# First attention: scores of the first tiles ahead of the value products, and batch two's six products in one round

## The reference

```python
mod = (_silu(L0_c) @ L0_wmod).reshape(2, 6, 1, -1)       # sa, ca, ga, sb, cb, gb
ga = (2 * (ga >= 0) - 1) * jnp.maximum(jnp.abs(ga), 0.25)
h = _layernorm(x) * (1 + ca) + sa
Q = h @ Wq.T + bq;  K = h @ Wk.T + bk;  V = h @ Wv.T + bv # 128 wide, one head
attn = softmax(where(causal, Q @ K.T / sqrt(128), -inf))
x = x + ga * (attn @ V)
```

## Time and profile before

| what | value |
|---|---|
| profiled execution, device time | 973.75 us |
| its span | 972.0 us |
| median of three runs | 973.2 us (969.73 to 974.66) |
| TensorE busy | 909.9 us, 94% |
| ScalarE, VectorE, GpSimd busy | 642.2, 593.1, 292.5 us |
| first attention, from the first q product to the last tile | 16.7 to about 82.5 us |

### The profile page before, as it was taken

The page is one execution under the profiler, slowest core; times in us unless marked ns, Lnnn a source line. Parts: engine busy times, 40 slices in busy tenths (PEclk is TensorE's granted clock), DMA queues, the critical chain, the costliest instruction groups (busy, mean ns, idle before and its releaser), DMA issues. The chain is left out here.

```text
span 972.0 us, 25390 instructions
## 1 busy us (share of the span) xinstructions
PE 909.9 (94%) x10211; PEld 668.2 (69%) x10211; DVE 593.1 (61%) x1355; ACT 642.2 (66%) x1094; POOL 292.5 (30%) x367
## 2 busy tenths in 40 slices
PE   7998897369999999999999999999999999998987
PEld 6676576146777767777776777777677777776776
DVE  5556111566666666666666666666666666677975
ACT  2552143158787878778787878778787877884442
POOL 5124800503224242422324142232414223215110
PEclk9998799569999999999999999999999999999999
DMA  8300701100020002002000200100020010000000
GB/s 251 137 2 22 254 26 52 40 1 2 2 90 3 2 2 92 2 2 84 9 3 1 91 2 2 76 17 2 2 91 1 3 31 10 3 1 2 1 23 22
DMA packets 27128, 35.48 MB, mean 37 GB/s; under 512 B 6042, under 2 KB 21716, under 8 KB 26836
## 3 DMA queue, kind: packets, MB, share of 16 engines
q1 hardware_dynamic: 25988, 31.76, 10.0%
q0 software_dynamic: 1024, 2.10, 0.7%
HBM read 28.48 MB, written 5.37 MB: 35 GB/s over the span
## 5 line engine op out<-in xcount | busy, mean ns | idle before, releaser
L552 DVE CUSTOM_DVE_ANT_0 soft<-SC,strips 128x1024 f32<-128x1024 f32 x256 | 303.3, 1223 | 79.7 <-PE SC L394 79.6
L513 ACT ACTIVATE soft<-soft,nmax 128x1024 f32<-128x1024 f32 x256 | 294.1, 1150 | 3.5 <-DVE nmax L552 3.4
L430 PE MATMUL CX<-PTs,V 128*64 128x256 f32 x2048 | 244.7, 381 | 0.0
L498 ACT COPY PTs<-PT 128x1024 f32<-128x1024 f32 x128 | 129.6, 1013 | 139.2 <-PE PT L413 139.2
L394 PE MATMUL SC<-qk 64*128 64x512 f32 x1536 | 212.5, 409 | 7.0 <-DVE nmax L552 6.9
L413 PEld LDWEIGHTS PT<-ident,soft 64*128 64x128 f32 x4096 | 159.0, 139 | 70.2 <-issue 28.9
L430 PEld LDWEIGHTS CX<-PTs,V 128*64 128x64 f32 x2048 | 142.6, 137 | 92.8 <-issue 35.0
L560 DVE COPY PTs<-PT 128x512 f32<-128x512 f32 x128 | 88.5, 692 | 161.0 <-PE PT L413 161.0
L413 PE MATMUL PT<-ident,soft 64*128 64x64 f32 x4096 | 176.4, 226 | 3.9 <-ACT PTs L505 2.4
L394 PEld LDWEIGHTS SC<-qk 64*128 64x128 f32 x1536 | 137.8, 188 | 32.9 <-issue 5.2
L341 POOL CAST qk<-raw_qk 128x512 fp32r<-128x512 f32 x60 | 36.8, 614 | 262.3 <-ACT raw_qk L317 262.3
(11 more groups left out here) (268 smaller groups left out, 998.2 us busy)
## 6 DMA issues: line engine op xcount, KB each, us to landing
strips<-bias_vec SPq DMA_DIRECT2D x8, 1920.0 KB, 7.0
arena<-in_L_ffn_w SPq DMA_DIRECT2D x1, 2048.0 KB, 11.3
slots_in<-arena SPq DMA_DIRECT2D x1, 1536.0 KB, 9.3
arena<-slots_in SPq DMA_DIRECT2D x8, 192.0 KB, 4.5
slots_out<-arena SPq DMA_DIRECT2D x8, 192.0 KB, 2.0
x<-in_L_attn_x SPq DMA_DIRECT2D x2, 512.0 KB, 4.4
out<-x SPq DMA_DIRECT2D x4, 256.0 KB, 2.3
arena<-in_L_wmod SPq DMA_DIRECT2D x2, 384.0 KB, 4.8
```

The lines of the kernel that those rows point to most:

```text
L430: ins = pe.matmul(CX[hd * DK:(hd + 1) * DK, 0:2 * P], V1[:, vb, t, hd * DK:(hd + 1) * DK], PTs[:, g % 2, hd, t, :], start=(t == 0), stop=( ...
L498: act.copy(turned_out(n, 0), turned_in(0)).then_inc(ev("ptA_out"), 1)
L513: act.activation(soft[:, n % RING, hd, :], soft[:, n % RING, hd, :], ACT.Exp, bias=nmax[:, j:j + 1], scale=-1.0, accum_out=rsum[:, hd, n % ...
L552: dve.tensor_tensor_reduce(soft[:, n % RING, hd, :], SC[hd][:, :], strips[:, u // B % 2, hd, i * P:i * P + S], 1.0, 3.4e38, ALU.add, ALU.m ...
```

## The change

- TensorE: scores 0, 1, 2, the transposes of tile 0, scores 3 and the transposes of tile 1 stand ahead of products 2 and 5 (both values of batch one). Products go in the order 0, 1, 3, 4, 2, 5, 6, ..., 11, and the waits of the other engines follow this order through `issued0`. Then come context 0, the transposes of tile 2, the row transposes of batch two, context 1, and products 6 to 11 in one go; from i = 5 on the loop is as before.
- Banks: product 2 goes to the fourth half bank instead of the first, product 9 to the third, 10 to PT[1], 11 to the second. Product 9 waits for the maximum of the third tile, 10 and 11 for the copies of q and k that were in their banks.
- The modulation helper is split in two. The vectors are made behind the first row transposes, not in front of them. ScalarE's row copy of the first half comes ahead of its copies of the vectors.
- Warm-up products: 3 instead of 6 behind the small rows' transpose, none instead of 4 behind the weights' transposes, none instead of 2 between the first two row transposes.
- VectorE: the modulation columns are copied ahead of the first normalised rows. Maxima 0 to 2, quarter three of the rows, maximum 3, quarter four, values 2 and 5, the additions of tiles 0 and 1, values 8 and 11, then the loop from i = 4.
- ScalarE: exponentials 0, 1, 2, copy of transposes 0, exponential 3, copies 1 and 2, then batch two's row copies and its q and k copies.

```diff
--- before.py
+++ after.py
@@ -230,9 +230,11 @@
 
 
         fills0 = [(kind, b, half) for b in range(B) for half in range(2) for kind in "qkv"]
-        fill_banks = [PT[0], PT[1], four_sc[0], CX[:, :], MI[:, :], four_sc[1],
-                      PT[1], four_sc[1], four_sc[3], PT[1], four_sc[1], four_sc[3]]
+        fill_banks = [PT[0], PT[1], four_sc[3], CX[:, :], MI[:, :], four_sc[1],
+                      PT[1], four_sc[1], four_sc[3], four_sc[2], PT[1], four_sc[1]]
         order0 = list(range(TB)) + list(range(NT - 1, TB - 1, -1))
+
+        issued0 = (0, 1, 3, 4, 2, 5, 6, 7, 8, 9, 10, 11)
 
         def width0(i):
 
@@ -840,7 +842,7 @@
                 for f, (kind, fb, half) in enumerate(fills0):
                     if kind == "v" or fb != b:
                         continue
-                    act.wait_ge(ev("proj0_full"), f + 1)
+                    act.wait_ge(ev("proj0_full"), issued0.index(f) + 1)
                     dst = (q0T if kind == "q" else k0T)[:, b * S + half * 512:b * S + half * 512 + 512]
                     if kind == "q":
                         ins = act.activation(dst, fill_banks[f], ACT.Identity, scale=-QK_SCALE, bias=cols[:, C_BQS:C_BQS + 1])
@@ -864,19 +866,25 @@
                 act.copy(tmp[:, at:at + width0(j) // P, :].rearrange("p k q -> p (k q)"),
                          PTW[:, 0:width0(j)]).then_inc(ev("pt0_out"), 1)
 
+            norm_out(0, (0,), (0,))
             mod_out(0)
-            norm_out(0, (0,))
+            norm_out(0, (0,), (1,))
             act.wait_ge(ev("bq_scaled"), 1)
             fills_out(0)
-            for i in range(NT + 2):
+            exp0(0)
+            exp0(1)
+            exp0(2)
+            turned0(0)
+            exp0(3)
+            turned0(1)
+            turned0(2)
+            norm_out(0, (1,))
+            fills_out(1)
+            for i in range(4, NT + 2):
                 if i < NT:
                     exp0(i)
-                if i >= 2:
+                if i >= 5:
                     turned0(i - 2)
-                if i == 2:
-                    norm_out(0, (1,))
-                if i == 3:
-                    fills_out(1)
                 if i == 14:
                     norm_out(1, (0,))
             norm_out(1, (1,))
@@ -1032,7 +1040,7 @@
                 kind, b, half = fills0[f]
                 t0 = b * TB + 4 * half
                 dve.wait_ge(ev("gate0_folded"), 1)
-                dve.wait_ge(ev("proj0_full"), f + 1)
+                dve.wait_ge(ev("proj0_full"), issued0.index(f) + 1)
                 tt(v0[:, t0:t0 + 4, :], fill_banks[f].rearrange("p (t d) -> p t d", d=D), bc_tiles(bvg[:, b, :], 4),
                    ALU.add).then_inc(ev("v0_out"), 1)
 
@@ -1066,14 +1074,12 @@
             silu()
             dve.wait_ge(ev("var_ready"), 1)
             inverse_roots(tiles(0))
+            mod_columns(0)
             rows_out(quarter(0), rows0)
-            mod_columns(0)
             rows_out(quarter(1), rows0)
             norm_stats(0, (1,))
             dve.wait_ge(ev("var_ready"), 2)
             inverse_roots(tiles(1))
-            values0(2)
-            rows_out(tiles(1), rows0)
             dve.wait_ge(ev("consts"), 8)
             ts(base_b, iota_c, 1.0 / P, None, ALU.mult).then_inc(ev("base_ready"), 1)
 
@@ -1119,16 +1125,23 @@
 
                 return bank[:, 0:n * E].rearrange("p (t e) -> p t e", e=E)
 
-            for i in range(NT):
+            biased0(0)
+            biased0(1)
+            biased0(2)
+            rows_out(quarter(2), rows0)
+            biased0(3)
+            rows_out(quarter(3), rows0)
+            values0(2)
+            values0(5)
+            added0(0)
+            added0(1)
+            values0(8)
+            values0(11)
+            for i in range(4, NT):
                 biased0(i)
-                if i == 1:
-                    values0(5)
-                if i >= 3:
+                if i >= 5:
                     added0(i - 3)
-                if i == 3:
-                    values0(8)
-                    values0(11)
-                if 4 <= i != 11:
+                if i != 11:
                     stats0(i - 4)
                 if i == 10:
                     stats0(7)
@@ -1367,27 +1380,28 @@
             keep_clock(PT[0], 6)
             pe.wait_ge(ev("ld_rows"), 16 * 8)
             pe.transpose(MI[:, 0:NROWS], rows[0:NROWS, :], ident[0:NROWS, 0:NROWS]).then_inc(ev("rows_turned"), 1)
-            keep_clock(PT[0], 6)
+            keep_clock(PT[0], 3)
             pe.wait_ge(ev("ld_w0"), 48)
             for n in range(3):
                 ins = pe.transpose(SC[0][:, n * P:(n + 1) * P], w0raw[:, n, :], ident[:, :])
             ins.then_inc(ev("w0_turned"), 1)
-            keep_clock(PT[0], 4)
-
-            def mod_rows(layer):
+
+            def mod_columns(layer):
 
                 for n, m in enumerate((0, 1, 3, 4)):
                     ins = mm(MI[:, 64 + 2 * n:66 + 2 * n], wmod[layer][:, m * D:(m + 1) * D], siluT[:, 2 * layer:2 * layer + 2],
                              start=True, stop=True)
                 ins.then_inc(ev("modc_full"), 1)
+
+            def mod_vectors(layer):
+
                 for b in range(B):
                     mm(four_sc[(2, 3, 1, 3)[2 * layer + b]], siluT[:, 2 * layer + b:2 * layer + b + 1].to_broadcast([P, P]),
                        wmod[layer][:, 2 * D:6 * D], start=True, stop=True).then_inc(ev("mod_full"), 1)
 
             pe.wait_ge(ev("silu_ready"), 1)
             pe.wait_ge(ev("ld_wmod"), 16)
-            mod_rows(0)
-            keep_clock(PT[0], 4)
+            mod_columns(0)
 
             def turn_rows(n, k):
 
@@ -1397,9 +1411,10 @@
                     ins = pe.transpose(rows_bank(n, k)[:, t * P:(t + 1) * P], rows_in[:, 4 * k + t, :], ident[:, :])
                 ins.then_inc(ev("h_turned"), 1)
 
+            keep_clock(PT[0], 4)
             pe.wait_ge(ev("w0T_ready"), 1)
             turn_rows(0, 0)
-            keep_clock(PT[0], 2)
+            mod_vectors(0)
             turn_rows(0, 1)
 
             def fill(f):
@@ -1407,12 +1422,16 @@
                 kind, b, half = fills0[f]
                 at = b * S + half * 512
                 pe.wait_ge(ev("hT_ready"), 2 * b + half + 1)
+                if f == 2:
+                    pe.wait_ge(ev("mod_copied"), 2)
                 if f == 8:
                     pe.wait_ge(ev("hT_ready"), 4)
                 if f == 6:
                     pe.wait_ge(ev("qk0_out"), 2)
-                if f >= 9:
-                    pe.wait_ge(ev("v0_out"), 3) if kind == "v" else pe.wait_ge(ev("qk0_out"), 5 if kind == "q" else 6)
+                if f == 9:
+                    pe.wait_ge(ev("nmax0"), 3)
+                if f >= 10:
+                    pe.wait_ge(ev("qk0_out"), f - 5)
                 if kind == "v":
                     pe.wait_ge(ev("gate0_folded"), 1)
                     for t in range(4):
@@ -1429,15 +1448,14 @@
                 if i == 0:
                     pe.wait_ge(ev("mod_copied"), 2)
                     pe.wait_ge(ev("qk0_out"), 2)
-                if i == 1:
-                    pe.wait_ge(ev("v0_out"), 1)
                 if i >= 2:
                     pe.wait_ge(ev("nmax0"), i - 1)
                 if i == 4:
-                    pe.wait_ge(ev("qk0_out"), 4)
-                    pe.wait_ge(ev("v0_out"), 4)
+                    pe.wait_ge(ev("qk0_out"), 7)
+                    pe.wait_ge(ev("v0_out"), 3)
                 if i == 5:
                     pe.wait_ge(ev("qk0_out"), 8)
+                    pe.wait_ge(ev("v0_out"), 4)
                 for k in range(0, w, 512):
                     m = min(512, w - k)
                     ins = mm(scores_bank0(i)[:, k:k + m], q0T[:, t * P:(t + 1) * P], k0T[:, b * S + k:b * S + k + m],
@@ -1458,6 +1476,7 @@
                 pe.wait_ge(ev("pt0_out"), j + 1)
                 if j < 2:
                     pe.wait_ge(ev("qk0_out"), j + 3)
+                    pe.wait_ge(ev("v0_out"), 1)
                 else:
                     pe.wait_ge(ev("att0_out"), j - 1)
                 n = width0(j) // P
@@ -1497,24 +1516,30 @@
                          skip_group_check=True)
                 ins.then_inc(ev("ranks_full"), 1)
 
-            for f in range(5):
+            for f in (0, 1, 3, 4):
                 fill(f)
-            for i in range(NT + 3):
+            for i in range(3):
+                scores0(i)
+            turn0(0)
+            scores0(3)
+            turn0(1)
+            fill(2)
+            fill(5)
+            context0(0)
+            turn0(2)
+            pe.wait_ge(ev("v0_out"), 2)
+            turn_rows(0, 2)
+            turn_rows(0, 3)
+            context0(1)
+            for f in range(6, 12):
+                fill(f)
+            for i in range(4, NT + 3):
                 if i < NT:
                     scores0(i)
-                if i == 1:
-                    fill(5)
-                if 2 <= i < NT + 2:
+                if 5 <= i < NT + 2:
                     turn0(i - 2)
```

(12 more changed lines are left out.)

## The result

The changed kernel takes 966.69 us in the median of six runs (965.64 to 968.43), the kernel before 972.46 (969.73 to 974.66, six runs). The ratio is 0.9942, with a 95% interval of 0.9925 to 0.996: 0.6% faster, 5.8 us. The profiled execution has 968.43 us in all and a span of 966.7, against 973.75 and 972.0.

What follows compares the result with a forecast made beforehand. TensorE's waits before the sixth tile's scores (the mark) were taken as the bound; moving the mark 4.9 us plus 0.25 later gave 5.15 off 973.75, 968.6, stated as 968.3 against the median. Likeliest range 966.5 to 970, wider 965.5 to 972.3.

Steps and rivals of the forecast that it cites:

- The bound: First attention: TensorE sets the pace from the sixth tile's scores (the mark, 39.76 us) to 80.60; before that it waits.
- The start: Opening: column products from 9.1 us, clock rising at about 15.5, vectors copied by 16.95, GpSimd's chain ending at 23.5.
- Scores ahead: First attention: scores 0 at 20.1 us, value products from 23.7, GpSimd wait hidden behind scores 0 to 3.
- VectorE as the new cover: Before batch two: VectorE is late next; quarter three 1.5 us, quarter four 1.06, values 2 and 5 done at 27.2.
- Banks: Products 9 to 11 do not wait; fifth tile's scores come at 33.9 us instead of behind VectorE's last copy, done at 34.8.
- The last term of the sum: Behind the mark: the fourth tile's transposes no longer wait 0.27 us for ScalarE, gaining 0.25 more.
- The shift one for one: A shift of the mark reaches the program's end in full; phases behind 80 us count nothing, 1.5 us allowed each side.
- The clock never rose as early as before: Opening, rival: the clock rises as before, the start is 1.3 us earlier, 967.0 us; chance 0.13.
- The fall in a new hole: TensorE between 22 and 27 us, rival: the clock falls in new holes, costing 1.7 us, 970.0; chance 0.11.
- Rows held by every GpSimd operation: VectorE's quarters three and four, rival: every GpSimd operation holds rows, 3.2 us more, 971.5; chance 0.10.
- Gain given back: Router and scatter, rival: the gain is lost as clock and queues shift, 973 us; chance 0.07.
- Slower: Opening, rival: without warm-ups TensorE stays at 1.2 GHz, 14 us lost less 5.15, 982 us; chance 0.07.

Runs made afterwards that it cites:

- the quiet kernel: Changed kernel with GpSimd's feed-forward gate made only after the sixth tile's maximum: 962.95 us, ratio 0.9952 to the kernel before.
- order only: Changed kernel with the old start and its warm-ups, keeping the new order of scores, products and banks: 965.63 us, ratio 0.9965 to the kernel before.
- the start alone: Kernel before with split modulation, fewer warm-ups, row copy and columns first, but old order and banks: 969.37 us, ratio 1.0009 to the kernel before.
- the slower comparisons: Groups of runs in which the kernel before takes 972 or 974 us; in the faster ones it takes 968 and 967.

## Why the prediction was right, point by point

**The number.** The forecast was 968.3, with 966.5 to 970 as the likeliest's own range; 966.69 was measured. Of the 1.6 us between them 0.7 is the kernel before, whose median is 972.46 over six runs and was 973.2 over three. The rest is the shift: 4.9 forecast, 5.8 measured, of which, as below, about 4.7 is the change's own.

**The bound.** Right: TensorE's pace from the mark on (38.95 of 40.71 us), waits before it. A shift of the mark did carry through; with its size see below.

**The start.** Right in kind, short in size. I had the rise of the clock at 15.5; it came at 16.9, the vectors ran slow to their end (3.58 instead of 2.7) and were copied at 17.58 instead of 16.95. That is the clock alone: the column products (8.98, forecast 9.1) and the vectors (13.38, forecast 13.5) began on time, although TensorE could turn the first small rows only at 6.50, against 5.95 before. GpSimd's chain took 6.5 as expected. Other executions were kinder: the five profiles of kernels with this start and these banks have the mark at 35.79, 35.42, 34.72, 34.12 and 35.00, mean 35.0 (the quiet kernel, which differs in GpSimd alone, has 34.92). The predicted 34.9 was right for the kernel, and 0.9 early for the execution that was shown.

**Scores ahead.** Right: scores 0 at 20.67 (20.1), value product at 24.25 (23.7), no wait on GpSimd. I had no wait for ScalarE's first copy as such; it is 0.67.

**VectorE as the new cover.** Right, and shown by the largest hole, 0.99, which VectorE releases. Quarter three took 1.83 (1.5), quarter four 1.10 (1.06), the two values end at 27.6 (27.2). That products of GpSimd hold the rows and tensor-scalar operations don't is shown by the quiet kernel (quarter three 1.71, four 1.03) and by order only (2.76 beside three products).

The Trainium skill, "SBUF — State Buffer", section "Who interferes with whom", counts a `tensor_scalar` of VectorE among those that can contend and says that issue order decides who blocks. The runs agree for GpSimd's tensor-tensor operations (2.76 for four rows) and show next to nothing for its tensor-scalar ones (1.10 against 1.03).

The forecast had these products come back at about 26, just behind quarter four (25.8), and they came at 26.70. What it did not say is that this rests on the new start, which *shifts* them there. By the mark the new order alone gains 2.4 us (37.17), the start alone loses 1.0 (40.64), and together they gain 4.6. Of the order's 37.17, 1.4 is the low stretch behind its longer hole. By the ratios the order alone is worth 0.35%, the start alone nothing or a loss of up to 0.2%, and together they give 0.5%. So the parts do not add; by how much is open, with one profile of each part and marks of one opening up to 1.7 us apart.

**Banks.** Right: 0.9 us, by the old banks, at the mark. The last term of the sum, 0.25 for a wait on ScalarE behind the mark, came out at half: from the mark to VectorE's last addition it is 42.78 us before and 42.65 after, 0.13 less, and the second profile of each agrees (42.78, 42.64).

**The shift one for one.** The term that I took for nothing, with 1.5 us allowed to each side, the phases behind 80 us, is not nothing in any one profile. From the last addition to the slot numbers it took 14.5 to 18.0 us over ten profiles with the same instructions there, the kernel before's two profiles 15.6 and 18.0, the changed kernel's 17.0 and 17.3. So neither the 1.4 that the first pair of profiles gave back in the router nor the 2.6 that it won behind the experts belongs to the change. Means of the mark are 39.6 before (two profiles) and 35.0 after (the five above): 4.6 us or 0.47%, and 4.7 with the 0.13. The two ratios, 0.9942 and 0.9954, hold this in their intervals. That the spans' 5.3 came so close to the predicted 5.15 is in part luck.

**Rivals.** The clock never rose as early as before (about 12) in the eight profiles without the nine warm-ups: their vectors began at 13.0 or later and still ran in part at the low rate. The earliest mark was 34.1, not 33.6; the kernel with the warm-ups back had the early rise and 34.5. The fall in a new hole happened with the order alone, not in the changed kernel. Rows held by every GpSimd operation: out, by the quiet kernel. Gain given back: only by chance. Slower: nowhere near; the slow rate lasted to 16.9, not through the opening.

## What to carry to other kernels

Fill a wait for a slow engine with work that doesn't need it, and then look at who is next: here VectorE, whose cost depended on when GpSimd's tensor-tensor products ran beside it, so that a part of the change that gains nothing by itself moved that run out of the other part's way. Split a gain between two profiles by stages, and profile each kernel twice before any stage behind the edit is explained: one stage with the same instructions differed by 3.5 us here, nearly what the change is worth. And a filled hole or an earlier semaphore is no gain where the next transfer runs into another one.

## What the runs showed of the hardware that was not expected

- ScalarE stood 3.9 us with no releaser at the opening of the second attention in all four profiles without warm-ups there from the slower comparisons, and in none of the eight from the faster ones. With 39 warm-up products on TensorE just before, in the slower setting, it was 12.7 us in two kernels. GpSimd issues gathers all through this stretch (one each 1.25 us, to between 184.5 and 190), and the wait ends 2 to 3 us behind the last of them each time. What ScalarE waited for was not found, and the 39 products weren't tried in the faster setting.
- The clock's rise at the start comes at another point in each execution of the same kernel (the four vector records take 3.58 and 3.01 in the changed kernel's two profiles), and so do the later low stretches: at 0.50 from 188 to 194 and from 201 to 208 us in the first, from 193 to 203 in the second. Between kernels with the same opening the mark moved by up to 1.7 us (34.1 to 35.8).
